# ctx's first load moved behind the four quarters of x, and a quarter of its first fold moved to VectorE

## What is computed

```python
x = x + autocorrelation(layernorm(x), ctx, ctx)     # (8, 512, 2048), 8 heads
x = x + expert_ffn(layernorm(x))                    # 64 experts of rank 8, top 16

def autocorrelation(Q, K, V):                       # per batch, per channel
    qf, kf = fft(q, axis=L), fft(k, axis=L)
    corr = ifft(qf * conj(kf)).real
    w, idx = top_k(corr, 12); w = softmax(w)
    out[l] = sum_i w[i] * v[min(idx[i] + l, L - 1)]
```

## Time and profile before

| | us |
|---|---|
| median of 3 runs | 2169.17 (2168.03 to 2170.2) |
| the profiled execution | 2167.58 |
| its span, first to last instruction | 2165.4 |
| TensorE busy | 2118.6 (98%) |
| VectorE busy | 1678.5 (78%) |
| GpSimd busy | 1565.5 (72%) |
| ScalarE busy | 1317.6 (61%) |

### The profile page before, as it was taken

The page is one execution under the profiler, slowest core; times in us unless marked ns, Lnnn a source line. Parts: engine busy times, 40 slices in busy tenths (PEclk is TensorE's granted clock), DMA queues, the critical chain, the costliest instruction groups (busy, mean ns, idle before and its releaser), DMA issues.

```text
span 2165.4 us, 29201 instructions
## 1 busy us (share of the span) xinstructions
PE 2118.6 (98%) x8920; PEld 1327.4 (61%) x8920; DVE 1678.5 (78%) x4046; ACT 1317.6 (61%) x2948; POOL 1565.5 (72%) x1024
## 2 busy tenths in 40 slices
PE   5999999999999999999999999999999999999999
PEld 2455455455455454454454454788888888888887
DVE  7999999999999999999999999744444444444443
ACT  4776776776776776776765646654444455445441
POOL 6999999999999999999999988533343433333420
PEclk9999999999999999999999999999999999999999
DMA  7232332333333332332221246444444444444431
GB/s 283 93 107 102 122 108 102 122 107 103 121 107 103 122 107 102 122 107 102 102 88 64 83 177 240 147 166 166 170 165 172 162 166 163 160 166 168 168 113 59
DMA packets 110416, 287.49 MB, mean 133 GB/s; under 512 B 7136, under 2 KB 7264, under 8 KB 109280
## 3 DMA queue, kind: packets, MB, share of 16 engines
q1 hardware_dynamic: 110304, 286.19, 37.6%
HBM read 219.06 MB, written 67.11 MB: 132 GB/s over the span
## 4 chain that ended last, share of the span: by engine, by line
PE 83%; POOL 6%; DVE 6%; issue 2%; ACT 2%; DMA 1%; SPq 0%; DVEq 0%; POOLq 0%; ACTq 0%
PE pair L739 13%; PE pair L733 8%; PE out L566 5%; PE out L568 5%; PE out L567 5%; PE z L568 5%; PE z L567 5%; PE z L566 5%; PE evac L616 5%; PE pair L629 4%; PE lag L683 4%; PE evac L640 4%; PE evac L641 4%; PE pair L729 3%; PE tp L585 2%
## 5 line engine op out<-in xcount | busy, mean ns | idle before, releaser
L1796 POOL TENSOR_TENSOR rows<-rows,cin 128x1024 f32<-128x1024 f32 x48 | 114.9, 2394 | 342.3 <-DMA rows<-out_dram 278.7
L739 PE MATMUL pair<-r_f,back 128*128 128x512 f32 x768 | 344.7, 597 | 7.4 <-DVE prod L1013 3.9
L1732 POOL TENSOR_TENSOR r_f<-prod 128x1024 f32<-128x1024 f32 x128 | 303.0, 2379 | 7.3 <-DVE prod L1011 5.0
L739 PEld LDWEIGHTS pair<-r_f,back 128*128 128x128 f32 x768 | 142.4, 190 | 202.2 <-issue 144.2
L733 PE MATMUL pair<-w_sb,wts 128*128 128x512 f32 x512 | 225.2, 593 | 2.0 <-DVE w_sb L1151 1.0
L566 PE MATMUL out<-b_hi,zt_hi 128*128 128x512 f32 x508 | 201.1, 396 | 2.7 <-ACT zt_hi L1637 1.5
L568 PE MATMUL out<-b_hi,zt_lo 128*128 128x512 f32 x508 | 198.2, 390 | 0.0
L567 PE MATMUL out<-b_lo,zt_hi 128*128 128x512 f32 x508 | 197.8, 389 | 0.0
L566 PE MATMUL z<-a_hi,xt 128*128 128x512 f32 x496 | 195.9, 395 | 0.0
L1421 ACT ACTIVATE xn<-tp 128x512 f32<-128x512 f32 x94 | 55.2, 587 | 230.4 <-PE tp L585 230.3
L568 PE MATMUL z<-a_hi,xt 128*128 128x512 f32 x496 | 193.3, 390 | 0.0
(11 more groups left out here) (229 smaller groups left out, 5546.7 us busy)
## 6 DMA issues: line engine op xcount, KB each, us to landing
out_dram<-att_sb SPq DMA_DIRECT2D x32, 1024.0 KB, 4.2
rows<-out_dram SPq DMA_DIRECT2D x64, 512.0 KB, 3.8
out_dram<-rows SPq DMA_DIRECT2D x64, 512.0 KB, 2.7
cin<-out_dram SPq DMA_DIRECT2D x63, 512.0 KB, 4.0
xin<-in_x_dram SPq DMA_DIRECT2D x63, 512.0 KB, 4.0
vf<-in_ctx_dram SPq DMA_DIRECT2D x31, 1024.0 KB, 5.1
xf<-in_x_dram SPq DMA_DIRECT2D x30, 1024.0 KB, 5.4
stat_in<-in_x_dram SPq DMA_DIRECT2D x27, 1024.0 KB, 5.1
```

The source lines that it names most:

```text
L739: return nc.tensor.matmul(pair_ps[:, bank, :], back[:, 3 * bank + n, :], r_f[:, row, :], start=n == 0, stop=n == 2)
L1732: nc.gpsimd.tensor_tensor(dst, prod[:, slot, 0:2, :], prod[:, slot, 2:4, :], ALU.add).then_inc(add_done, 1)
L1796: nc.gpsimd.tensor_tensor(half, first, other, op).then_inc(c_added, 1)
```

## The change

The load of ctx's first tile is issued behind all four quarters of x, in place of between the second and the third. Of the four operations of its fold, GpSimd keeps three; the fourth (the differences of the second stage, into `vf[2:4]`) is done by VectorE between `first_normalizers` and `first_fold`, after a wait for `v_half`. It raises a new semaphore, `first_rest`, and TensorE waits for it in step 0 beside `v_ready`, which GpSimd now raises after its third operation.

```diff
-        v1_loaded = sem("v1_loaded")
+        v1_loaded, first_rest = sem("v1_loaded"), sem("first_rest")
...
             for q, buf in enumerate((e[:], pick[:], p_f[:], r_f[:, 4:8, :])):
                 load_stat(-2, q, buf, start_loaded[q])
-                if q == 1:
-                    load_v(-1, 1, 0)
+            load_v(-1, 1, 0)
             sp.dma_start(fwd[:].rearrange("p n m -> p (n m)"), tables["fwd"]).then_inc(fwd_loaded, 16)
...
                 def ctx_cyclic():
                     pe.wait_ge(v_ready, i + 1)
+                    if is_step(i, 0):
+                        pe.wait_ge(first_rest, 1)
...
             first_normalizers()
+            dve.wait_ge(v_half, 1)
+            first = prod[:, 1, :, :]
+            nc.vector.tensor_tensor(vf[:, 2:4, :], first[:, 0:4:2, :], first[:, 1:4:2, :], ALU.subtract).then_inc(first_rest, 1)
             first_fold()
...
             pool.wait_ge(v_half, 1)
-            nc.gpsimd.tensor_tensor(vf[:, 0:2, :], first[:, 0:4:2, :], first[:, 1:4:2, :], ALU.add)
-            nc.gpsimd.tensor_tensor(vf[:, 2:4, :], first[:, 0:4:2, :], first[:, 1:4:2, :], ALU.subtract).then_inc(v_ready, 1)
+            nc.gpsimd.tensor_tensor(vf[:, 0:2, :], first[:, 0:4:2, :], first[:, 1:4:2, :], ALU.add).then_inc(v_ready, 1)
```

## The result

| | before | changed |
|---|---|---|
| median of 20 runs, us | 2168.81 (2167.43 to 2170.58) | 2171.72 (2170.01 to 2174.11) |
| span of the profiled execution, us | 2165.4 | 2168.2 |

The ratio is 1.0014, 95% interval 1.0007 to 1.002: 2.9 us slower. The interval lies above 1 and reaches just to 0.2%: a loss that is real and small.

A forecast was written before the change was run, and what follows sets the result against it. The first 50 us were bound by the wait chain through x's last load, normalizing, x's fold and GpSimd. x's path +2.66, tied with TensorE, was taken as +2.75: 2169.17 + 2.75 = 2171.9 us, range 2169.2 to 2174.5.

The forecast's parts named there:

- The loads, and the overlap: x's last statistics begin 2.70 us earlier, so VectorE's small operations meet GpSimd's ctx folds and wait them out.
- rival 2: Small VectorE operations pass GpSimd's folds, only large ones exclude each other: +2.3, 2171.5 us; chance 0.13.
- rival 3: No VectorE and GpSimd operations exclude each other at the start: +1.1, 2170.3 us; chance 0.05.
- rival 4: Nothing excludes anything and TensorE's clock rises by 26.6, so the product follows x: -0.8, 2168.4 us; chance 0.03.
- The sum on VectorE and ScalarE: Small operations held behind GpSimd's folds put ScalarE's first normalizing of x at 24.34, +2.66 in place of -2.70.
- The VectorE fold: VectorE's new ctx fold, some 1.2 us from 24.3 to 25.5, is hidden under ScalarE before x's fold at 25.90.
- TensorE: TensorE starts at 25.6 against 20.95, and its twelve instructions before the first product end at 33.4.
- The rise of the clock: TensorE's clock goes from 1.2 to 2.4 GHz at 30.1 to 30.8, say 30.4.
- two paths that I called tied: Before the first product, TensorE's path (33.4) and VectorE's (33.36) tie; product at 33.4 to 33.6, +2.7 to +2.9.
- rival 1: TensorE's clock rises later; with all twelve instructions at 1.2 GHz +5.5, 2174.7 us, slower by over 0.2%; chance 0.10.
- the sign to look for: 51.93 on TensorE (its second tile) moves by 2.7, and the end with it; otherwise the prediction is wrong.
- Rival 5: The later start is taken up before the steady state: +0, 2169.2 us; chance 0.06.

The follow-up runs named there:

- experiment 3: The changed kernel with one operand of each of the four small VectorE operations in PSUM in place of SBUF; median 2172.79 us, ratio 1.0016.
- experiment 5: The changed kernel with GpSimd's three ctx folds also waiting until the small VectorE operations are done; median 2173.68 us, ratio 1.0019.
- experiment 6: The changed kernel with each of GpSimd's three ctx folds split into two operations of 512 columns; median 2171.58 us, ratio 1.0011.
- experiment 7: The changed kernel with five matmuls of tables ahead of TensorE's first ctx matmul; median 2171.02 us, ratio 1.0012.
- changed kernel with its wait filled: The changed kernel with two matmuls of tables in TensorE's 2.1 us wait at about 65 us; median 2170.47 us, ratio 1.0010.
- kernel before with its wait filled: The kernel before with two matmuls of tables in TensorE's wait at about 65 us; median 2167.59 us, ratio 0.9996.
- filled pair: The changed kernel and the one before, each with two matmuls of tables in TensorE's wait at about 65 us; 2170.47 against 2167.59 us.
- fold only: The kernel before, its load order kept, with only the fourth ctx fold moved to VectorE; median 2169.21 us, ratio 1.0003.

## Why the prediction was right

**The loads, and the overlap.** Right. The statistics came at 11.39 and 14.11 (11.4, 14.1), L924's successor lasted 1.06 (near 1) and the next 2.26 (over 2). What no row of before showed, whether 4 elements are held as 2048 are, is shown by experiments 3, 5 and 6: yes, if both operands are in SBUF, and until the GpSimd instruction that runs has ended. Rivals 2 (small operations pass) and 3 and 4 (nothing excludes anything) are refuted by the three lengths alone.

**The sum on VectorE and ScalarE.** Right in its mechanism, 0.19 too long: ScalarE started at 24.15, not 24.34. I let the last held operation start where the fold ends (23.95) and take its own 0.16 from there. It ended with the fold (23.91 beside 23.90), and the fold itself ended 0.05 sooner. All later terms carry this: x's fold 25.70 (25.90), GpSimd 30.95 (31.14).

**The VectorE fold.** Right: 24.03 to 25.25, hidden under ScalarE (0.45 us were left before x's fold).

**TensorE.** The start was right (25.39, forecast 25.6). The rise of the clock was not: I took 4.5 to 5.2 us after the start and so 30.4. The weight loads of the changed kernel, from TensorE's timeline:

```profile
28.12 0.30 PEld L617 LDWEIGHTS evac<-vf,fwd 128*128 128x128 f32 x1 [0.55 <-ACT v_cyc L1470]
28.94 0.21 PEld L617 LDWEIGHTS evac<-vf,fwd 128*128 128x128 f32 x1 [0.52 <-issue]
29.81 0.30 PEld L617 LDWEIGHTS evac<-vf,fwd 128*128 128x128 f32 x2 [0.66 <-ACT v_cyc L1470]
30.92 0.30 PEld L630 LDWEIGHTS pair<-xf,fwd 128*128 128x128 f32 x2 [0.81 <-DVE xf L943]
```

The load at 28.94 lasts 0.21, near the 0.19 of the high level, so the rise came by then, some 3.6 us after the start. TensorE even waited 0.81 us for x. The two paths that I called tied were not in this execution, the product started on VectorE's time (33.17), and experiment 7 shows that TensorE could have been quicker without effect. In the changed kernel with its wait filled the rise did come near 30.4 (a load of 0.30 at 29.78, the next of 0.19 at 30.39). x's matmuls began at 31.25 there, and four of 0.43 with the tail of 0.2 end at 33.2, level with the product at 33.16: with that rise the tie is as forecast. Where the rise came later against x's path, at about 30 us in experiment 3 and after 31.1 in experiment 6, VectorE did wait 0.74 and 1.34 us for TensorE. So rival 1 (the rise comes late) did not decide the changed kernel, but it names what moved those two marks.

**What became of it later.** At the mark the shift was +2.46 where I had +2.75 (and 2.7 as the sign to look for); the mechanism held and the size was 0.3 too large. At the end it was +2.8. The stores of results are later by 2.45 at first (100.5 us before), by 2.64 from about 300 us on, and by 2.85 to 2.89 from 1074 us on. So the forecast's 2.75 was 0.3 too much at the start, and 0.4 of drift that it had not, made up for it: that the total came so close is in part luck. The drift comes in two steps, at the sixth store (304 us) and at 1074 us. The changed kernel with its wait filled has both (2.45 to 2.61, 2.52 to 2.73), and so has the one of experiment 7, while the kernel before with its wait filled has neither (-0.01 to -0.02, -0.06 to -0.05). So they belong to the kernel. Another drift belongs to an execution: behind 1300 us the filled kernel before goes from -0.06 to -0.36 against before, where both run the same code. The cause of either stays open. Rival 5 (the shift is taken up) is out, since no store moved by less than 2.45.

**The chances.** 0.86 for within 0.2% against a ratio of 1.0014. By the filled pair the distance to the bound is 1.4 us, so that was fair.

## What to carry to other kernels

Before you move a transfer, look what the engine that consumes it runs beside afterwards: ctx's folds cost nothing while VectorE took statistics (one input), and with the loads' gain set against it 4.7 us beside four operations of 4 elements each with two SBUF operands. VectorE and GpSimd are one resource for such operations, and a tiny one on the path waits out the GpSimd operation beside it. The way out is an operand in PSUM, or all of the work on the faster engine: VectorE with three folds more was 2.8 us quicker. And look for lengths that a row should not have; a hold of this kind appeared as busy time in every row here, not as idle time.

## What the runs showed of the hardware

**Who gets in.** A VectorE operation that waits gets in between two GpSimd operations: those of the changed kernel ended at 19.20 and 21.49, though GpSimd's next fold stood right behind the one before (19.14, 21.56). Likewise GpSimd gets in between two of VectorE (experiment 3: 1.23, then 3.38 on GpSimd, then 2.83 on VectorE). Neither engine kept the other out for longer than one operation.

**The rise of TensorE's clock varies.** From the first matmul to steps of 0.43 it took 3.6 us in the changed kernel, some 4.6 to 5 in fold only and with operands in PSUM, and 5.6 to 6.1 in experiments 6 and 7 (the first load of 0.19 at 31.63 and 25.14), the latter busy without a gap. The Trainium skill (TensorE: Matmul & The Clock Gate, "What's actually happening") says that the number of slow matmuls differs between runs of the same kernel; the traces agree, with the same start in the changed kernel and in the one with its wait filled: near the high level at 28.94 in one (a load of 0.21), still low at 28.89 in the other (0.34).

**A wait of 2.1 us** of TensorE within a busy stretch was followed by a fall of the clock in some executions, 14 of 35 of before by their mean clocks, and in none of 34 where two matmuls filled it. In the profiles the granted clock was 0.66 of 65 to 70 us in fold only, 0.50 of 70 to 75 us with folds in halves. In fold only it put the first weights matmul 1.24 us later (68.90 against 67.66) where the mark had moved 0.05.
